# A four-layer graph network on one core: part of the edge sums begun while the rows are still scattered, a shorter first stage, and the last update moved into the last edge pass

## What is computed

```python
h0: edge_aggr = zeros.at[src].add(edge_attr).at[dst].add(edge_attr)
    relu(concat([h, edge_aggr]) @ W1 + b1) @ W2 + b2
h1: agg = segment_sum(edge_attr, dst)
    relu(concat([h, agg]) @ W1 + b1) @ W2 + b2
h2: two graph convolutions, each sum of dinv[src] * dinv[dst] * (h @ W)[src] by dst, with a relu between
h3: messages = relu(concat([h[src], h[dst], edge_attr]) @ msg_w1 + msg_b1) @ msg_w2 + msg_b2
    aggregated = segment_mean(messages, dst)
    relu(concat([h, aggregated]) @ upd_w1 + upd_b1) @ upd_w2 + upd_b2
```

## Time and profile before

| what | us |
|---|---|
| median of 3 runs (1463.71, 1464.97, 1466.68) | 1464.97 |
| the profiled execution, its own time | 1461.87 |
| its span on the core | 1460.0 |
| first stage | 22.6 |
| scatter stage | 536.1 |
| sums stage | 126.6 |
| flags, check of the general path | 9.0 |
| dense layers, convolutions, tables | 210.0 |
| edge pass | 526.7 |
| its last collects, check, update, last store | 29.0 |

### The profile page before, as it was taken

The page is one execution under the profiler, slowest core; times in us unless marked ns, Lnnn a source line. Parts: engine busy times, 40 slices in busy tenths (PEclk is TensorE's granted clock), DMA queues, the critical chain, the costliest instruction groups (busy, mean ns, idle before and its releaser), DMA issues. The chain is left out here.

```text
span 1460.0 us, 32667 instructions
## 1 busy us (share of the span) xinstructions
PE 1248.2 (85%) x9632; PEld 906.7 (62%) x9633; DVE 880.1 (60%) x2762; ACT 554.3 (38%) x1458; POOL 808.4 (55%) x844
## 2 busy tenths in 40 slices
PE   5888888888888887887789998999988898988986
PEld 3555555555555556886469996477766666666664
DVE  6777777787877876665785448244444433443434
ACT  5444544444445447940241104233322222222221
POOL 5777777777777771000000001777777777777770
PEclk9999999999999999999799998899999999999996
DMA  7533335333333325875500003655555555455422
GB/s 230 135 104 106 104 108 148 101 104 104 103 108 108 102 67 177 240 240 162 48 1 2 1 2 105 166 153 154 158 155 154 154 151 142 136 149 142 134 75 56
DMA packets 198505, 174.71 MB, mean 120 GB/s; under 512 B 48724, under 2 KB 171078, under 8 KB 198246
## 3 DMA queue, kind: packets, MB, share of 16 engines
q1 hardware_dynamic: 171752, 118.36, 30.1%
q0 software_dynamic: 26624, 54.79, 13.0%
HBM read 134.89 MB, written 38.16 MB: 119 GB/s over the span
## 5 line engine op out<-in xcount | busy, mean ns | idle before, releaser
L2132 POOL DMA_INDIRECT between<-p_table,src_g x416 | 397.2, 955 | 474.1 <-DMA p_table<-n_nm 347.6
L380 PE MATMUL acc<-ones_b 128*128 128x512 bf16 x1606 | 426.3, 386 | 31.4 <-PEq L1396 12.4
L765 POOL DMA_INDIRECT rows_by_block<-h_t,mean_bc x312 | 299.8, 961 | 109.7 <-issue 77.4
L380 PEld LDWEIGHTS acc<-ones_b 128*128 128x128 bf16 x1606 | 142.5, 99 | 132.6 <-issue 39.0
L917 PE MATMUL acc<-n_nm 128*128 128x384 bf16 (+1 forms) x832 | 140.8, 291 | 86.6 <-DVE n_nm L817 85.8
L2204 ACT ACTIVATE between<-acc 128x256 f32<-128x256 f32 x208 | 79.8, 383 | 355.3 <-PE acc L2252 348.2
L849 DVE TENSOR_TENSOR between<-between,acc 128x600 f32 x208 | 161.3, 775 | 61.5 <-issue 49.8
L2163 DVE TENSOR_TENSOR between<-acc,between 128x256 f32<-128x256 f32 x208 | 87.8, 422 | 169.2 <-DMA between<-p_table,src_g 108.6
L2277 PE MATMUL acc<-w_msg,between 128*128 128x128 f32 x832 | 185.5, 305 | 0.0
L2263 PEld LDWEIGHTS acc<-between 128*128 128x128 f32 x832 | 129.6, 198 | 82.6 <-issue 58.9
L2263 PE MATMUL acc<-between 128*128 128x24 f32 x832 | 134.6, 243 | 49.5 <-DVE agg_sum L2172 49.0
(11 more groups left out here) (194 smaller groups left out, 1942.7 us busy)
## 6 DMA issues: line engine op xcount, KB each, us to landing
h_t<-rows_by_block SPq DMA_DIRECT2D x73, 387.0 KB, 3.7
between<-in_edge_attr SPq DMA_DIRECT2D x207, 128.0 KB
h_t<-in_edge_attr SPq DMA_DIRECT2D x78, 256.0 KB
between<-in_dst SPq DMA_DIRECT2D x51, 288.0 KB
between<-p_table,src_g POOLq DMA_INDIRECT x416
agg_sum<-in_edge_attr SPq DMA_DIRECT2D x25, 256.0 KB
rows_by_block<-h_t,mean_bc POOLq DMA_INDIRECT x312
rows_by_block<-x_nm SPq DMA_DIRECT2D x1, 4644.0 KB, 18.6
```

The source lines that it names most:

```text
L380: pe.matmul(acc[:, bank * BANK:(bank + 1) * BANK].rearrange("p (a n) -> p a n", n=P), ones_b[:, :], ones_b[:, :].rearrange("p (a n) -> p a ...
L765: pool.indirect_dma_start(rows_by_block, bass.IndirectOffsetOnAxis(ap=place_in_table[:, t:t + 1], axis=0), row_group(g)[:, j, :], None).th ...
L2132: pool.indirect_dma_start(got[:, q, j * D:(j + 1) * D], None, p_table, bass.IndirectOffsetOnAxis(ap=src_g[:, n * G + j:n * G + j + 1], axi ...
```

## The change

It has three parts.

**Chunks.** While the scatter goes on, the first 3 tiles (384 rows, `CROWS`) of each block of the table are read back and summed as soon as enough rows must be there: 72 chunks, chunk m being tiles 3 (m // 24) on of block m % 24. SP loads chunk m with group m+32, ScalarE makes its one-hots with group m+29, TensorE sums it with group m+30, VectorE takes it with group m+31 into `home`, with a copy for the first chunk of a block and an addition for the others. SP runs ahead of the other engines in this stage, as it loads the rows for eight groups later. Counters read out three times (`counts_at`) show afterwards whether the chunks were full. The warm-up products now come behind the ranks and go to the pair's own bank. The sums stage reads only what is left: 50 reads, 225 tiles. The load of x moves into it, `home` and the sum by destination are added there, and ScalarE looks through 14 blocks of counts and the union (bitwise or, on VectorE) of the other eleven.

**First stage.** The row loads of groups 4 to 7 move to the next block, GpSimd clears 26 pieces of 400 words without its two waits, ScalarE clears 9600 words of `between` instead of 7800, and 12 warm-up products are left of 16.

**Last update.** The windows' path is entered once, with everything from the dense layers to the end inside it; the general path's blocks come all behind it, in one. The update of 256 nodes (`NODES_AT`) runs inside the edge pass two turns later, in eleven chunks; three blocks of 128 nodes are left for its end. A new check asks whether each pair's window begins early enough for that. In the last turn the collects are put ahead of the last additions where they can be.

The diff, cut to its core:

```diff
+CT = 3
+CROWS = CT * P
+CRING, CHOTS = 3, 2
+CHUNK_LOAD, CHUNK_HOT, CHUNK_SUM, CHUNK_TAKE = 32, 29, 30, 31
+CHUNKS = EC // KC - CHUNK_LOAD
...
-        POOL_FIRST, POOL_SECOND = 2800, 9400
+        POOL_PIECE, POOL_PIECES = 400, 26
...
-                for g in range(EARLY, ROWG):
-                    load_group(sp, g)
...
-                clear(between_words[:, POOL_FIRST + POOL_SECOND:])
+                clear(between_words[:, POOL_PIECE * POOL_PIECES:])
...
-                pool.wait_ge(vec.h, vec.at(6))
-                pool.memset(between_words[:, 0:POOL_FIRST], 0.0)
-                pool.wait_ge(idx_read.h, idx_read.at(1))
-                pool.memset(between_words[:, POOL_FIRST:POOL_FIRST + POOL_SECOND], 0.0)
+                for k in range(POOL_PIECES):
+                    pool.memset(between_words[:, k * POOL_PIECE:(k + 1) * POOL_PIECE], 0.0)
...
-                stream_ones(pe, LAST_BANK, WARM_UP)
+                stream_ones(pe, LAST_BANK, WARM_SHORT)
...
+                    def load_chunk(m):
+
+                        if m >= CRING:
+                            sp.wait_ge(chunk_summed.h, chunk_summed.at(m + 1 - CRING))
+                        row = m % (NB - 1) * CAP + m // (NB - 1) * CROWS
+                        sp.dma_start(chunk_rows[:, m % CRING, :, :], rows_by_block[row:row + CROWS, :].rearrange("(p j) w -> p j w", j=CT))\
+                          .then_inc(chunk_in[m % CRING].h, 16)
+
+                    for g in range(EARLY, ROWG):
+                        load_group(sp, g)
                     for g in range(ROWG, GROUPS):
...
+                        if g >= CHUNK_LOAD:
+                            load_chunk(g - CHUNK_LOAD)
...
+                    def hots_of_chunk(m):
+                        act.wait_ge(chunk_in[m % CRING].h, chunk_in[m % CRING].at(16 * (m // CRING + 1)))
+                        if m >= CHOTS:
+                            act.wait_ge(chunk_summed.h, chunk_summed.at(m + 1 - CHOTS))
+                        h = chunk_hot[:, m % CHOTS, :, :]
+                        for j in range(CT):
+                            act.activation(h[:, j, :], iota[:, :], ACT.Abs, scale=-1.0, bias=chunk_rows[:, m % CRING, j, D:KW]).then_inc(chunk_away.h, 1)
+                        act.wait_ge(chunk_away.h, chunk_away.at(CT * (m + 1)))
+                        act.activation(h, h, ACT.Relu, scale=-1.0, bias=ones[:, 0:1]).then_inc(chunk_hots.h, 1)
...
+                        if i % PG == 1 and 0 <= g - CHUNK_HOT < CHUNKS:
+                            hots_of_chunk(g - CHUNK_HOT)
...
+                    def take_chunk(m):
+                        dve.wait_ge(chunk_summed.h, chunk_summed.at(m + 1))
+                        at = home[:, m % (NB - 1) * P:m % (NB - 1) * P + P]
+                        o = IDLE_BANK * BANK
+                        if m < NB - 1:
+                            dve.tensor_copy(at, acc[:, o:o + P]).then_inc(chunk_taken.h, 1)
+                        else:
+                            dve.wait_ge(chunk_taken.h, chunk_taken.at(m + 2 - NB))
+                            dve.tensor_tensor(at, at, acc[:, o:o + P], ALU.add).then_inc(chunk_taken.h, 1)
...
                         if i % PG == 1 and g + 1 < GROUPS:
                             own_rank(g + 1)
+                        if i % PG == 1 and 0 <= g - CHUNK_TAKE < CHUNKS:
+                            take_chunk(g - CHUNK_TAKE)
...
+                    def sum_chunk(m):
+                        pe.wait_ge(chunk_hots.h, chunk_hots.at(m + 1))
+                        if m >= 1:
+                            pe.wait_ge(chunk_taken.h, chunk_taken.at(m))
+                        o = IDLE_BANK * BANK
+                        for j in range(CT):
+                            last = pe.matmul(acc[:, o:o + P], chunk_rows[:, m % CRING, j, 0:D], chunk_hot[:, m % CHOTS, j, :],
+                                             start=j == 0, stop=j == CT - 1)
+                        last.then_inc(chunk_summed.h, 1)
+
                     rank(0)
                     for i in range(PAIRS):
                         g, q, c = i // PG, i // PG % ROWG, i % PG * 2
-                        stream_ones(pe, IDLE_BANK, WARM_UP if i % WARM_EVERY == WARM_EVERY - 1 else WARM_PAIR)
                         if c == 0 and g + 1 < GROUPS:
                             rank(g + 1)
+                        with_chunk = c == 0 and 0 <= g - CHUNK_SUM < CHUNKS
+                        if with_chunk:
+                            sum_chunk(g - CHUNK_SUM)
+                        if i >= PRING:
+
+                            pe.wait_ge(taken.h, taken.at(i + 1 - PRING))
+                        stream_ones(pe, at_bank(i) // BANK, WARM_UP if i % WARM_EVERY == WARM_EVERY - 1 else WARM_CHUNK if with_chunk else WARM_PAIR)
...
-                stream_ones(pe, LAST_BANK, WARM_SHORT)
                 pe.wait_ge(vec.h, vec.at(1))
...
+                stream_ones(pe, LAST_BANK, WARM_SHORT)
...
+                        if j == 0 and nodes_at(it, i, UPD_FIRST) is not None:
+                            pe.wait_ge(averaged.h, done_at(averaged, it))
+                            pe.matmul(acc[:, update_bank(i):update_bank(i) + NODES_AT], w2_msg[:, :], mean_of, start=True, stop=True)
+                        if j == 0 and nodes_at(it, i, UPD_SECOND) is not None:
+                            pe.wait_ge(hidden.h, done_at(hidden, it))
+                            for b in range(NODES_AT // P):
+                                pe.matmul(acc[:, update_bank(i) + b * P:update_bank(i) + b * P + P], hidden_of[:, b * P:b * P + P], w2_upd[:, :], start=True, stop=True)
...
-        with path(FAST):
+        with when_in_windows():
+            two_dense()
             convolve_by_counts()
             sum_window_messages()
         with general():
+            general_sums()
+            two_dense()
             convolve_by_gather()
             node_tables()
             sum_block_messages()
+            update()
```

More of the change, by code:

```diff
@@ L165, in _, with when_in_windows @@
                 def _(eng):
[L166 to L170, removed]
-            return wrap
+                    f(eng)
+            return wrap
+        @contextmanager
+        def when_in_windows():
+            taken_here = nc.values_load(flags[0:1, FAST:FAST + 1], min_val=0, max_val=1)
+            with nc.If(taken_here), path(FAST):
+                yield
         @contextmanager
@@ L649, in build @@
         pair_done = signal("pair_done")
+        chunk_in = [signal(f"chunk_in{q}") for q in range(CRING)]
+        chunk_away = signal("chunk_away")
+        chunk_hots = signal("chunk_hots")
+        chunk_summed = signal("chunk_summed")
+        chunk_taken = signal("chunk_taken")
         taken = signal("taken")
@@ L883, in _ @@
                     dve.tensor_tensor(over[:, 1, :], bases[:, GROUPS % 2, 0:NB], bounds[:, 1, :], ALU.is_gt)
+                    for c, n in enumerate(BY_CHUNK):
+                        dve.tensor_tensor(over[:, 2 + c, 0:n], counts_at[:, c, 0:n], bounds[:, 2 + c, 0:n], ALU.is_lt)
                 @on(block.tensor)
@@ L937, in place_and_count @@
             away_made.passed(EC)
-            loaded.passed(16 * 23)
+            for s in (chunk_hots, chunk_summed, chunk_taken):
+                s.passed(CHUNKS)
+            chunk_away.passed(CT * CHUNKS)
+            for q in range(CRING):
+                chunk_in[q].passed(16 * len(range(q, CHUNKS, CRING)))
+            loaded.passed(16 * 21)
             vec.passed(2)
@@ L1089, in sum_blocks @@
                 n = (CAP if b < NB - 1 else CAP_LAST) // P
-                for j in range(0, n, LR):
-                    reads.append((b, b * CAP + j * P, min(LR, n - j), j == 0, j + LR >= n))
+                done = CT * sum(b < k for k in BY_CHUNK)
+                for j in range(done, n, LR):
+                    reads.append((b, b * CAP + j * P, min(LR, n - j), j == done, j + LR >= n))
             last_read = {read[0]: r for r, read in enumerate(reads)}
+            STATS_FROM = 4 * LB_IN
+            AVERAGES_FROM = STATS_FROM + -(-NB // 2)
+            assert AVERAGES_FROM + -(-NB // 2) <= len(reads)
             with nc.Block(no_gpsimd_drain=True) as block:
@@ L1218, in build, with general_sums @@
         sums.passed(1)
-        with general():
+        def general_sums():
             with nc.Block(no_gpsimd_drain=True) as block:
@@ L2058, in steps_of @@
                 body(0, True, False)
-                with eng.Fori(1, loops - 1) as it:
+                body(1, False, False)
+                body(2, False, False)
+                with eng.Fori(3, loops - 1) as it:
                     body(it, False, False)
                 body(loops - 1, False, True)
+                if tail is not None:
+                    tail()
+                    return
                 for i in range(RING, RING + max(lag for _, lag in lagged)):
@@ new lines, in last_of_pairs @@
+                    def last_of_pairs():
+                        it = loops - 1
```

(11 more changed lines are left out.)

339 lines of the change are left out of this document (234 added, 105 removed).

## The result

The changed kernel takes 1769.22 us (median of 4 runs, 1767.15 to 1772.23) against 1465.83 for the kernel before: a ratio of 1.207 (95% interval 1.204 to 1.210). It was forecast slower, 1728 us, range 1602 to 1800. Its profiled execution has a span of 1770.3 us, 310.3 more than before.

What follows compares the result with a forecast made beforehand. The scatter stage was taken as bound by a chain between TensorE, VectorE and GpSimd. Scatter +343, first stage -6.5, sums -48, checks -5.3 and tail -18.7 gave +264, so 1728 us, range 1602 to 1800.

Steps and rivals of the forecast that it cites:

- The period in series: Scatter stage: TensorE's chunk sum waits for VectorE's previous take, so a group takes 8.31 us against 5.04; +232 us over 71 groups.
- The clock: Scatter stage: TensorE's stand of 3.9 us drops its clock in each of 71 groups, +1.7 us a fall, +121 us.
- GpSimd's room: Scatter stage: GpSimd, with 25% to spare, would follow the longer group period.
- C: Rival, chance 0.07: TensorE doesn't stand at the chunk sum because the take is already done; total 1377 us.
- the -10: Scatter stage: the other 33 groups gain 0.3 us each, as ranks come ahead of the warm-ups; -10 us.
- The first stage: First stage: row loads move out and ScalarE's clearing sets the end, 16.1 us instead of 22.6; -6.5 us.
- it waits for one piece: First stage: VectorE waits for one 400-word GpSimd memset piece, 0.34 us, and is done some 6 us sooner.
- The sums stage: Sums stage: 225 of 441 tiles stay, 78 us instead of 126.6; -48 us, bounds -57 and -40.
- DMA 71 us: Sums stage: 16.5 MB left to read, at 231 GB/s, take DMA 71 us.
- Checks: Flags and path checks: falling through into the windows' path saves 3.7 us, two dropped checks per block 1.6.
- The tail: From the last gather to the end: fewer blocks left to update, path check beside the store's landing; -18.7 us.
- The edge pass: Edge pass: GpSimd sets its pace and hides the update's eleven chunks; 0, or +11 if late waits reach it.

Runs made afterwards that it cites:

- warm_in_wait: The changed kernel with twelve more warm-up products per chunk group on TensorE, ahead of its wait for the take, which stays: 1603.27 us.
- take_mid_iteration: The changed kernel with VectorE's take moved from the end of its odd iteration to the start, same group: 1588.59 us.
- take_same_group: The changed kernel with VectorE taking each chunk one group sooner, in the group where TensorE sums it: 1401.77 us, ratio 0.958 to the kernel before.
- small_reads: The changed kernel with the take one group sooner and sums-stage reads of 3 tiles, eight buffers: 1859.50 us against 1873.59 for the kernel before, ratio 0.991.

## Why the prediction was right, and where its terms were off

The direction, the mechanism and the range came out as argued. The chain was read from the counts of two semaphores in the code and one interval of the trace (L824 to L830), and each of its links is in the timeline of after: the release of the chunk products by the take, 71 times, 3.7 us on average and 4.1 at most. Its size was 41 us short of the measured time. Two sums of the text are off by 1 us, which changes nothing: 1726 + 3.1 is 1729, not 1728, and VectorE's addition and ORs in the sums stage come to 13.9 us by L1120's 951 ns for 768 words, not 12.9. By terms:

- **The period in series**: 8.31 us forecast, 8.21 measured where the clock holds (warm_in_wait). Close, in part by luck: an ordinary group takes 7.97, and the mean includes the five groups with 16 warm-ups, some 2.8 us longer each, of which the prediction said nothing. Against the 5.12 us of these groups before it is 219 us instead of 232.
- **The clock**: 1.7 us a fall forecast, 2.28 measured, 162 us instead of 121. The mis-sized term. The 1.7 was the price of one stretch of 3.4 us at half clock. Here nearly every fall in the record lasted 6.8 us, begun in part while TensorE still stood, and in the third of the clock rows above, the second 3.4 us of work, the mean is still 0.72. take_mid_iteration has both lengths, at 1.6 and 2.9 us a fall.
- **GpSimd's room**: "GpSimd had 25% to spare and follows" was a misreading, and the largest one. Its idle time in the scatter stage was "issue" already in the kernel before, which the same text read rightly for the edge pass. It did no harm to the forecast, as a period of 10 us hides it, but it made C too fast: of its 1377 the -10 isn't to be had, and take_same_group, the kernel of that rival, takes 1402. The 31 groups ahead of the first wait did gain, 4.42 us each against 4.94 before; in the changed kernel that counts (some 16 us, 10 forecast), in a kernel bound by GpSimd it does not.
- **The first stage**: -6.5 forecast, -0.5 measured. The step that failed is "it waits for one piece": the first cast waited for all of them, which none of the bounds (-2 to -6.9) had. The Trainium skill, "SBUF — State Buffer", "Who interferes with whom", has casts among the operations that can contend with GpSimd, and lets the loser wait for one whole instruction. The trace agrees that a cast is held up; it was held for the piece that was running and all 24 behind it. With the two waits the stage is over at 15.9, against the forecast's 16.1.
- **The sums stage**: -48 forecast, -35.5 measured, outside its own bound of -40. "DMA 71 us" took 231 GB/s for given; 182 came (the stage's row of the kernel after). The reads' size and number of buffers was the thing left out, and small_reads has the 73 us. Another 5 us of the 91 are absent in take_same_group (85.7), whose clock in the stage is 0.94 instead of 0.87; whether one brings the other was not tried.
- **Checks**: -3.9 us, -3.7 forecast. VectorE's waits there, kernel after:

```profile
DVE n_nm L1479 <- PEq L1310: 4.0, 1, 4.0
```

  The 4.0 us are no check any more: they are for TensorE's end of the block (L1310), which comes behind its twelve warm-ups (1013.7 on, 2.75 us). These stood ahead of the flags before and stand behind them now, in the path both times, a move that the prediction left uncosted. What went is the jump: from TensorE's last work ahead of it to VectorE's L1356 were 5.1 us, from the end of the warm-ups to L1479 are 0.9. The Trainium skill, "Advanced Engine Details and Errata", "Control Flow Timing", has 108 ns for a compare-and-branch; by that the stretch would have stayed within 0.2 us of what it was, and it is 3.9 shorter. The two later checks that were dropped gave nothing: that stretch grew by 1.8 us, the cause of which wasn't tried.
- **The tail**: -18.7 forecast, -13.9 measured. The end of kernel after:

```profile
1755.54 0.42 DVE L2341 TENSOR_TENSOR between<-acc,between 128x256 f32<-128x256 f32 x1
...
1757.65 0.18 DVE L2381 TENSOR_TENSOR agg_sum<-agg_sum,acc 128x24 f32 x1 [1.11 <-PE acc L2482]
...
1761.88 0.33 SPq L2292 DMA_DIRECT2D out<-x_nm  x1
```

  From the end of the last collect to the last store 4.05 us (2.9 forecast), and 8.4 from there to the end instead of 5.6: the jump was taken for 4.6 us beside the store's landing, and with what follows it it is longer (3.8 us of branch on TensorE and 3.3 behind it). The collects put ahead of the last addition also hold that addition up: it begins 4.3 us after the last gather is put out, 3.5 in the kernel before.
- **The edge pass**: 0 forecast, -0.6 measured: eleven chunks of update cost nothing under GpSimd's pace.

## What to carry to other kernels

Where two engines hand each other work in both directions, count for each wait which iteration of the other engine gives the release, and whether that iteration can begin before this engine has gone on; one group off here turned a gain of 4% into a loss of 21%. Idle time that says "issue" at the same 0.3 us before nearly every instruction belongs to a busy engine: here 0.96 + 0.30 us was the pace, and a busy share of 75% hid it. And a stage that is waiting for another engine pays twice if the wait is long enough for TensorE's clock to fall: a run with useless products in the wait tells the two prices apart.

## What was not expected of the hardware

- A row of 26 memsets (9.76 us in all) on GpSimd shut a cast of VectorE's out for 8.8 to 9.2 us in nine of ten runs, and for 4.67 in one; begun behind a wait, the same row let VectorE's operations through at a cost of up to 0.2 us each.
- A jump over the unused path took TensorE's branch 3.4 to 4.4 us, and what followed it up to 4.4 more; without the path the end came 5.5 us sooner.
- A stand of TensorE of 2.1 us was followed by half clock in some 40 of 71 cases, one of 3.7 us in all of them.
- On two chips TensorE, VectorE and ScalarE stopped together, mostly for 2 to 6 us, 15 to 30 us apart, in every kernel, while GpSimd went on for a time. Its cause is open.
